# A four-layer transformer kernel on one core: one VectorE instruction for the maxima of two heads over two PSUM banks, both banks refilled together

## The reference, cut to what matters

```python
# layer 0, 32-token blocks: later blocks get a score of 0, not minus infinity
scores = jnp.einsum('bihd,bjhd->bhij', q, k) / scale
scores = jnp.where(allowed, scores, jnp.zeros((), scores.dtype))
probs = jax.nn.softmax(scores, axis=-1)
ctx = jnp.einsum('bhij,bjhd->bihd', probs, v).reshape(B, S, H)
return ctx @ Wo.T + bo
# layer 1: causal, with a linear bias per head (ALiBi) and LoRA weights
s = jnp.einsum('bhqd,bhkd->bhqk', q, k) / jnp.sqrt(jnp.float32(dh)) + bias[None]
s = jnp.where(j[None, None] <= i[None, None], s, NEG_INF)
out = jnp.einsum('bhqk,bhkd->bhqd', jax.nn.softmax(s, axis=-1), v)
```

## Time and profile before

| what | value |
|---|---|
| time, median of 3 runs | 2217.85 us (2210.37, 2217.85, 2218.25) |
| the profiled execution: span from its first to its last instruction | 2215.5 us |
| TensorE matmul busy | 1867.7 us, 84% |
| VectorE busy | 1282.6 us, 58% |
| ScalarE busy | 1049.3 us, 47% |
| GpSimd busy | 712.8 us, 32% |
| maxima (L685) | 1536 instructions, 755.8 us |

### The profile page before, as it was taken

How to read it: one execution, slowest core, us unless ns; L and a number is a source line. 1 busy time by engine, 2 the same in 40 slices (tenths; PEclk the granted TensorE clock), 3 DMA queues, 4 the chain that set the end, 5 groups by cost and what they waited for, 6 DMA issues and landing times.

```text
span 2215.5 us, 34423 instructions
## 1 busy us (share of the span) xinstructions
PE 1867.7 (84%) x12909; PEld 864.2 (39%) x12909; DVE 1282.6 (58%) x2930; ACT 1049.3 (47%) x1768; POOL 712.8 (32%) x796
## 2 busy tenths in 40 slices
PE   2788788756569989998999999899999967999998
PEld 0233233224344555554444444333333324444443
DVE  1666666637767666673110111489989916776663
ACT  1266565532123655565222222188888854445432
POOL 3176666545532322220110011122233115443330
PEclk9799999867868999998899999799999978999999
DMA  8323343000023343220000002143223110000000
GB/s 195 66 58 67 71 87 65 1 11 1 1 57 59 68 89 77 59 59 2 2 0 1 0 1 57 26 89 60 59 58 81 36 48 1 1 10 5 6 5 15
DMA packets 70270, 91.58 MB, mean 41 GB/s; under 512 B 13228, under 2 KB 63772, under 8 KB 65228
## 3 DMA queue, kind: packets, MB, share of 16 engines
q1 hardware_dynamic: 64536, 84.42, 18.5%
q10 hardware_dynamic: 5568, 4.96, 0.7%
HBM read 49.10 MB, written 39.85 MB: 40 GB/s over the span
## 4 chain that ended last, share of the span: by engine, by line
PE 52%; issue 5%; DVE 5%; ACT 4%; DMA 2%; SPq 1%; POOL 1%; DVEq 0%; POOLq 0%; ACTq 0%
PE ps L1401 9%; PE ps L417 5%; DVE mx L685 3%; PE ps L2798 3%; PE ps L391 3%; PE ps L375 3%; PE ps L2078 2%; PE ps L403 2%; PE ps L2080 2%; PE ps L2096 2%; PE ps L353 2%; PE ps L330 2%; PE ps L1391 2%; DMA Qst<-mT 1%; PE ps L1771 1%
## 5 line engine op out<-in xcount | busy, mean ns | idle before, releaser
L685 DVE TENSOR_REDUCE mx<-ps 128x1 f32<-128x512 f32 (+3 forms) x1536 | 755.8, 549 | 255.8 <-PE ps L353 121.4
L593 ACT ACTIVATE Pr<-ps 128x1024 f32<-128x1024 f32 (+3 forms) x512 | 350.1, 705 | 233.0 <-PE ps L335 117.4
L586 ACT ACTIVATE Pr<-ps 128x512 f32<-128x512 f32 x512 | 274.6, 600 | 48.4 <-PE ps L391 43.1
L353 PE MATMUL ps<-Kst,Qst 63*128 63x512 bf16 (+3 forms) x1024 | 235.2, 326 | 60.8 <-DVE mx L685 38.2
L330 PE MATMUL ps<-Qst,Kst 64*128 64x512 bf16 (+3 forms) x1024 | 229.2, 324 | 48.6 <-issue 32.1
L375 PE MATMUL ps<-Pr,V 128*32 128x512 f32 (+3 forms) x2048 | 204.5, 473 | 4.4 <-ACT ctxU L599 3.1
L403 PE MATMUL ps<-Kst,Qst 63*128 63x512 bf16 x512 | 169.3, 401 | 6.6 <-DVE mx L685 4.4
L417 PE MATMUL ps<-Pr,V 128*32 128x256 f32 x2048 | 165.1, 394 | 8.4 <-ACT ctxU L599 7.5
L2826 POOL TENSOR_TENSOR ve<-mv,eps 128x4 f32<-128x4 f32 x41 | 8.8, 214 | 502.4 <-DVE mv L2815 502.4
L391 PE MATMUL ps<-Qst,Kst 64*128 64x512 bf16 x512 | 154.4, 388 | 14.9 <-issue 9.0
L1509 DVE SCALAR_TENSOR_TENSOR f_shared<-ps,w_L_s_w,f_own 128x512 f32<-128x512 f32 x32 | 23.4, 748 | 230.6 <-ACT f_own L1462 199.6
(11 more groups left out here) (342 smaller groups left out, 3355.5 us busy)
## 6 DMA issues: line engine op xcount, KB each, us to landing
Qst<-parts_scratch SPq DMA_DIRECT2D x48, 384.0 KB, 6.0
Kst<-parts_scratch SPq DMA_DIRECT2D x48, 384.0 KB, 8.4
parts_scratch<-qpart SPq DMA_DIRECT2D x48, 192.0 KB, 2.7
parts_scratch<-kpart SPq DMA_DIRECT2D x48, 192.0 KB, 2.7
parts_scratch<-qpart SPq DMA_DIRECT2D x48, 128.0 KB, 2.6
parts_scratch<-kpart SPq DMA_DIRECT2D x48, 128.0 KB, 2.7
parts_scratch<-qpart SPq DMA_DIRECT2D x48, 64.0 KB, 2.3
parts_scratch<-kpart SPq DMA_DIRECT2D x48, 64.0 KB, 2.3
```

Of the source, the lines that this page charges most:

```text
L353: mm = pe.matmul(ps[:, 4 + a, lo:lo + W], k.Qst[rows, n.par, pair, P * it:P * it + P], k.Kst[rows, n.par, pair, 0:W], start=True, stop=not ...
L586: act.activation(k.Pr[:, g % 2, 2 * (j // 2) + 1 - j % 2, :], ps[:, self.bank_t(b, g, j), :], ACT.Exp).then_inc(self.s_exp.sem, 1)
L593: act.activation(k.Pr[:, g % 2, 2 * tile:2 * tile + 2, 0:W], ps[:, 2 * tile:2 * tile + 2, 0:W], ACT.Exp).then_inc(self.s_exp.sem, 1)
L685: dve.tensor_reduce(k.mx[:, half, at:at + 1], ps[:, bank, lo:lo + W], AX_X, ALU.max, negate=True).then_inc(self.s_max.sem, 1)
```

## The change

In the causal kinds `maxima` takes the fills of the two heads in pairs. It waits until both banks are filled, and one `tensor_reduce` reads the same columns of banks 4 and 5 and writes two maxima, for head 0 and head 1. It adds 2 to the semaphore, so the counts stay as they were. `freed` changes with it: fills 0 and 1 of an even unit wait for all 8 maxima of the pair before, those of an odd unit for the 2 of the even unit, and fills 2 and 3 for 6. The order of the instructions on TensorE stays, and so does the third attention.

```diff
--- before.py
+++ after.py
@@ -282,6 +282,9 @@
 
     def freed(self, c, k):
 
+        if self.causal:
+            pair, phase = divmod(c, 2)
+            return 8 * pair + (0, 2 if k < 2 else 6)[phase]
         _, now = self.fills(c)
         a, u, _ = now[k]
         if k >= 2:
@@ -673,6 +676,17 @@
         def maxima(n, c):
             pair, fills = self.fills(c)
             half, i = divmod(pair, 4)
+            if self.causal:
+                for (_, u, its), _ in zip(fills[0::2], fills[1::2]):
+                    dve.wait_ge(self.s_scores.sem, self.s_scores.at(n, u + 2 * len(its)))
+                    if u % 32 == 0:
+                        dve.wait_ge(self.s_mT_ps.sem, self.s_mT_ps.at(n.plus(-1), half + 1))
+                    for it in its:
+                        W, lo = self.span(it), self.place(its, it)
+                        heads = k.mx[:, half, :].rearrange("p (a j) -> p a j", a=2)
+                        dve.tensor_reduce(heads[:, :, 4 * i + it:4 * i + it + 1], ps[:, 4:6, lo:lo + W], AX_X,
+                                          ALU.max, negate=True).then_inc(self.s_max.sem, 2)
+                return
             for a, u, its in fills:
                 dve.wait_ge(self.s_scores.sem, self.s_scores.at(n, u + len(its)))
                 if u % 32 == 0:
```

## The result

The changed kernel takes 2262.82 us (median of 4 runs, 2256.68 to 2267.78) against 2215.95 for the kernel before: ratio 1.0209, 95% interval 1.0186 to 1.0232. I had forecast 2228 with 2209 to 2241. The direction was right, the size was not. The profiled span grows from 2215.5 to 2265.9 us, by 50.4.

The account below looks back on a forecast made before the run. It took the hand-off of a bank filled, reduced and refilled as the bound, not VectorE's throughput. Losses of 0.94 and 0.3 us a batch, x 8, gave 7.5 and 2.4, total +10 us: forecast 2228, range 2209 to 2241.

Parts of the forecast that it names:

- rivals 2 (faster): Both heads' scores end together, so the shorter reduce chain decides: at most 14 us faster, 2204, or 2211; chance 0.12.
- 3 (all covered): The row of maxima and the splits take up every loss: no change, 2218 us; chance 0.18.
- rival 1: Rotation lost everywhere, no saving from the merge: 2237 us, or 2247 if slots 4 to 7 and 15 lose too; chance 0.20.
- which slots of a batch set its end: Second attention: slots 8 to 14 and 0 to 3 on the path; first: only slots 14, 15 and 0 to 3.
- Slot 15 has such a cover too: Second attention: waiting for slot 14's row of maxima hides what slot 15 loses; no loss was priced there.
- Slot 7's cover: Second attention: 1.67 us idle before slot 8's scores, waiting for a row of maxima, absorbs losses of slots 4 to 7.
- (a): Second attention, slots 3 and 11: both third fills wait for the merged reduces: 0.17 us each, 0.34 a batch.
- (d): Second attention, even to odd slot: head 0's fill waits for all 1024 columns: +0.22 us in slot 9, half, +0.11, in 1.
- (c): Second attention: third fills' longer reduce delays the next slot's first fills: 0.05 us in 1 to 2, 9 to 10, 13 to 14.
- (b): Second attention, slots with 512-wide context matmuls: the reduces start later, delaying the third fill: 0.12 us, counted in slot 13 only.
- The first attention, 0.3 us a batch forecast: First attention: about +0.05 us in slot 3, +0.10 in 1 to 2, +0.15 in 15; x 8 = 2.4 us.
- 0.07 a merge: VectorE time saved per merged reduce, read from the trace because successive reduces overlap; preferred to the skill's 0.125 us.

Follow-up runs that it names:

- split_batch0: Changed kernel, but batch 0 of both attentions keeps one reduce a head and a refill for each bank by itself: 2236.8 us, ratio 1.0107.
- apart_slot15: Changed kernel, but the odd unit of slot 15 in each batch keeps its single reduces and own refills: 2256.3 us, ratio 1.0182.
- apart_slot7: Changed kernel, but the odd unit of slot 7 in each batch keeps its single reduces and own refills: 2259.2 us, ratio 1.0192.
- both_unmerged: Changed kernel without the merge: one reduce a head and tile, but both of the changed kernel's waits kept: 2267.9 us, ratio 1.0228.
- fill3_last_warm: Kernel before with head 1's third fill moved behind the small step, plus spare 128-row matmuls in both openings: 2204.2 us, ratio 0.9927.
- warm_opening: Changed kernel plus spare matmuls using 64 array rows while batch 0's maxima run ahead: 2262.1 us, ratio 1.0203.
- warm_full_array: Changed kernel plus spare matmuls using all 128 array rows while batch 0's maxima run ahead: 2258.3 us, ratio 1.0188.

## Why the prediction was wrong

- The direction was right, and so was the mechanism of a bank's fill and reduce that no longer overlap; neither of the rivals 2 (faster) nor 3 (all covered) came about. The time landed beyond rival 1.
- What failed first is the step "which slots of a batch set its end". It priced one batch in the steady state and multiplied by 8. Batch 0's maxima run with nothing beside them, and there each of the three hand-offs a pair is on the path: 20.8 of 49 us, given back by split_batch0. The granted clock there was 0.68 (60 to 90 us) and 0.73 (660 to 700 us) before, a sign that this stretch differs; a look at one pair of it would have shown 3.66 of 4.61 us in reduces and the alternation at work.
- "Slot 15 has such a cover too": it was 0.33 us deep, and the loss in that slot is larger. +0.70 us a batch in place of 0, and 0.69 of it given back by apart_slot15. Slot 7's cover of 1.67 us held (apart_slot7): from slot 4 to 8 a batch takes 11.90 us before and after, and the idle time at slot 8 goes from 1.67 to 0.80.
- The terms (a) to (d) of the second attention, 0.94 us a batch in all, were mis-sized by a factor of two. Each term put to the pair that holds it, beside the medians of batches 1 to 6 before and after (slots 8 to 10 at the full clock):

| slots | terms | forecast | before | after | measured |
|---|---|---|---|---|---|
| 0 to 2 | (c) + half of (d) | 0.16 | 5.52 | 5.84 | 0.32 |
| 2 to 4 | (a) | 0.17 | 5.88 | 6.18 | 0.30 |
| 8 to 10 | (c) + (d) | 0.27 | 5.18 | 5.70 | 0.52 |
| 10 to 12 | (a) | 0.17 | 5.92 | 6.22 | 0.30 |
| 12 to 14 | (b) + (c) | 0.17 | 5.74 | 6.18 | 0.44 |
| sum | | 0.94 | | | 1.88 |

- For (a) the trace shows what was short. In slot 11 the first reduce starts 0.12 us behind the last addition's end (915.77 + 0.21 to 916.10) where I took 0.05, and the odd score matmul holds head 1's fill back by 0.18 where I took 0.16: +0.29 for the 0.17 taken. What made (b), (c) and (d) too small was not taken apart. With slot 15 it is 2.6 us a batch at the full clock.
- The first attention, 0.3 us a batch forecast, shows +1.1 as a mean and +0.5 as a sum of medians. The places were right, the sizes again too small: slots 14 to 4, forecast 0.30, show +0.75 (6.15, 5.18 and 5.19 us to 6.54, 5.47 and 5.26), and slots 4 to 14, forecast 0, go from 30.8 to 30.5, though inside them slots 8 to 10 are 0.95 us longer, at more of the half clock.
- Batch 7 shows +3.4 and +4.0 us where I took 0.3 and 0.9. The score fills' waits for reduces grow by as much (7.2 to 10.7 us and 1.1 to 5.2). It has no splits and no stacks to wait for, so I take it that it has no such cover; no run took it apart.
- The durations of the merged reduces and the 0.06 us from a reduce's end to the fill were right; VectorE's busy time fell by 34.5 us, just under the 36 to 77 given. The rule of the Trainium skill (VectorE: DVE Perf Modes, on the fixed latency per instruction) that I weighed against 0.07 a merge would have given 0.125: measured are 0.067 in busy time, and on the path 0.05 for a pair's four merges (both_unmerged against after).
- The rule of the Trainium skill (Perfetto Trace Analysis, Optimizing Tensor Performance) that independent groups should rotate through PSUM banks had no price in the page; the runs give it here: 21 us (traces) to 23 us (ratios) in the two openings, where nothing else covers, and about 24 in all the rest, which split_batch0 keeps (1.0107).

Open: why the clock halves after slot 8's idle time in some batches of the second attention and not in others is not settled; idle times of 1.67 us are followed by either, and in apart_slot15 so are idle times of 0.8 us.

## What to carry to other kernels

A merge of two instructions that ties two buffers together trades a fixed cost, here 0.07 us of VectorE's time and next to nothing on the path, for the alternation of fill and drain; price the alternation where nothing else runs (openings and ends of a loop) and not only in the steady state. A cover is a number: compare its depth in the trace with the loss it has to take, slot by slot. A fill that must wait could go later in its engine's order here without loss while its partner's buffer stayed in work, and with a loss of 16 us or more once both buffers waited together. An expected time that comes true doesn't show the expected place: look where the gain lies.

## What the runs showed of the hardware that I had not expected

TensorE's granted clock was 0.54 over 35 us in which the spare matmuls used 64 of the 128 rows and TensorE was busy 91% of the time, and 1.00 in the same stretch with spare matmuls of all 128 rows, busy 78%. A stretch of 5.18 us took 6.16 with the clock at half for 3.4 us of it and 7.98 with half for 6.8. One reduce over two PSUM banks takes about as long as its columns say: 1225 ns for 2 x 512, against an estimate of 1206 from 420 and 682 ns for 256 and 512 columns. The record of the granted clock can be wrong for a stretch: it reads 1.00 in split_batch0's first opening (60 to 90 us), where a context matmul takes 1.06 us as at the half clock before, and 0.59 to 0.62 at the full clock of fill3_last_warm; so the matmuls' own durations are the check. In the two kernels above they agree with the record: a spare matmul takes 0.63 us in warm_opening at the half clock and 0.38 in warm_full_array.
